# Capped expert layer with added rows, experts and combination as one program, and the last layer's stores issued from SyncE

## The chip, the cores and the metric

The kernel runs on one core of one Trainium2 chip. The metric is the device time of one execution in microseconds. Three runs of the kernel before gave 2523.3, 2524.7 and 2529.2 us, median 2524.7.

## The reference

A two-layer network on x of 32 x 64 = 2048 tokens of 256 float32 numbers. Six blocks are added to x in turn, each on the layer-normed x: attention over a compressed context, a state-space block, the **capped** mixture of experts, cross attention, self attention, and a second mixture (the **last layer**). The change touches the two mixtures:

```python
# capped: E=64 experts of width 176, K=6, CAP=128, a shared expert of width 352
scores = softmax(xf @ gate_w.T); _, idx = top_k(scores + gate_b, K)
weights = take_along_axis(scores, idx, 1)
# rows of an expert beyond its first 128 are dropped (pos < CAP)
h  = silu(xb[e] @ w1[e].T) * (xb[e] @ w3[e].T); yb = h @ w2[e].T
y  = zeros.at[tok].add(yb[slot] * weights);  z = silu(xf@ws1.T) * (xf@ws3.T) @ ws2.T
return y + z
# last: E=64 of width 128, K=8 out of 4 of 8 groups, no cap, weights normalised,
# a shared expert of width 128; same sum
```

## The kernel before

Tokens lie as 16 tiles of 128 rows in X (SBUF). Each stage is one or more programs; at the end of each, all engines meet. `stage_moe` builds both mixtures, each as three programs.

**Routing** (`r`, L1082 to L1359). VectorE normalises a tile, SyncE stores it to memory (xn), TensorE transposes it, ScalarE copies it out twice (xnT for the shared expert, xts for the logits), TensorE makes the logits. Two buffers alternate. VectorE then chooses the K experts of all tiles (MAX8, FIND_INDEX8) and writes one-hot rows `oh` (L1298); TensorE counts them with triangular and all-ones matrices (ranks, L1173); VectorE adds over the tiles (L1303), picks each choice's slot (L1320, L1321), and the **table** is made: for each of 16 x K pairs VectorE writes `atp` (L1337), VectorE or ScalarE writes `atb` (L1339, L1218, L1224, L1226, L1341) and TensorE adds the product (L1184). Out come `tok`, the token of each slot, and in the capped layer `dest`, the row k*2048 + token of its result; empty slots have token 0 and an out-of-range `dest`.

**Experts** (`x`, L1362 to L1518). A block is 128 slots of one expert: 64 blocks in the capped layer, 192 in the last one, of which those behind the filled ones are empty. Per block: SyncE loads the weights (w13, w2) eight blocks ahead (L1387 to L1390; in the last layer a register load of the expert's number first, L1386); GpSimd gathers the rows (L1406); TensorE transposes (L1433), multiplies to hidden (L1444) and to output (L1455; in the last layer L1458 behind a register load, L1457); ScalarE copies rows (L1469) and applies silu (L1475); VectorE multiplies (L1504) and copies the result to `yb` (L1514). The result goes to memory: in the capped layer by GpSimd's indirect scatter, six blocks later in its order (L1413), in the last layer from ScalarE's queue (L1483), behind a wait for `yb`. `in_steps` writes the order: within a step, the parts of later blocks stand first (turn b+2, hidden b+1, output b; on ScalarE rows b+2, gate b+1, store b).

**Combination** (`c`, L1521 to L1641). TensorE makes the shared expert's hidden rows in units of 128 x 512 (12 in the capped layer, 4 in the last; L1564) and its outputs per tile (L1578). VectorE makes the weights (L1609, L1611 and some small ones), adds the shared output (L1630), and for each tile K multiply-adds of the results (L1634), in the capped layer also the statistics of the next norm (L1641). The results come by plain loads (capped, L1544) or by indirect gathers on GpSimd, eight a tile, three tiles of buffers (last, L1553). SyncE stores the output (L1538).

In `stage_mla` SyncE clears the capped layer's result area of 12288 rows in 16 stores (L422).

Of the kernel before, what the change touches and what calls it, by code (L numbers as in the profile page):

```python
# [44 lines left out]
SLOTS0 = E * CAP0  # L45
NB1 = T * K1 // P + E
SLOTS1 = NB1 * P
# [24 lines left out]
def bc(ap, shape):  # L72
    return ap.broadcast_to(shape)
# [124 lines left out]
def stage_mla(nc, e, d):  # L198
# [12 lines left out]
    with st.ctx:  # L211
# [36 lines left out]
        NCL = 16  # L248
        clear = sb("clear", [P, T * K0 * D // (P * NCL)])
        y_clear = d["y0"].rearrange("(n p r) d -> n p (r d)", n=NCL, p=P)  # L250
# [164 lines left out]
        with nc.Block() as block:  # L415
            @block.sync
            def _(sp):

                for n in range(NCL):
                    if n < NT - 3:  # L420
                        sp.wait_ge(sem("x_added"), n + 1)
                    sp.dma_start(y_clear[n], clear[:, :]).then_inc(sem("y_clear"), 16)  # L422
                sp.wait_ge(sem("y_clear"), 16 * NCL)

# [623 lines left out]
def stage_moe(nc, e, d, layer):  # L1048
# [16 lines left out]
    xn, y = d[f"xn{layer}"], d[f"y{layer}"]  # L1065
    R = 8

    with st.ctx:
        xnT = sb("xnT", [P, KD, T])
        gslot = None if capped else sb("gslot", [P, NT, K], U32)  # L1070
        wts = sb("wts", [P, NT, K])
        tok = sb("tok", [P, NB_], U32)
        dest = sb("dest", [P, NB_], U32) if capped else None
        ebrow = sb("ebrow", [1, NB_], U32)
        ws13, ws2 = sb("ws13", [P, KD, 2, SI]), sb("ws2", [P, NSB, D])
        w2all = None if capped else sb("w2all", [P, E, D])
        sc = sb("sc", [P, NT, E])
        oh = sb("oh", [P, NT, K, E], BF16)
        slotf = sb("slotf", [P, NT, K])


        r = Stage(nc, f"m{layer}r")  # L1082
        rs = r.sem
        with r.ctx:
# [6 lines left out]
            NA = 2 * E if capped else NB_  # L1091
            ACT3 = 3
            if capped:
                destp, desti = r.sb("destp", [P, 2, NT, K]), r.sb("desti", [P, 2, NB_], I32)
                slotv = r.sb("slotv", [P, 3, NB_])
            else:
                far, ntok = r.sb("far", [P, NT, K]), r.sb("ntok", [P, NT])
                dist = r.sb("dist", [P, 2, NB_])
            ln = LayerNorm(r, e, r.ps("psT2", [P, 512]))
            xts = r.sb("xts", [P, 2, KD, P])  # L1100
# [4 lines left out]
            pr = r.sb("pr", [P, NT, K, E])  # L1105
            ltrib, onesb = r.sb("ltrib", [P, P], BF16), r.sb("onesb", [P, P], BF16)
            before = r.sb("before", [P, NT + 1, E])
            sloti = r.sb("sloti", [P, 2, NT, K], I32)
            place = r.sb("place", [P, 2, NT, K])
            HQ = 16  # L1110
            atp = r.sb("atp", [P, HQ, P], F16)
            atb = r.sb("atb", [P, HQ, NA], F16)
            nb = r.sb("nb", [P, 4, E])
            nbi = r.sb("nbi", [P, 2, E], I32)
            ebc = r.sb("ebc", [P, 2])
            gt8, gs = r.sb("gt8", [P, NT, NGR, 8]), r.sb("gs", [P, NT, NGR])
            gm = r.sb("gm", [P, NT, NGR])
# [4 lines left out]

            def by_scalar(n):

                return capped or n % ACT3 == ACT3 - 1

            def act_count(n):

                return n if capped else n // ACT3
# [4 lines left out]
            if capped:  # L1134
                LOADS.append((destp[:, :, :, :], d["dest_parts"]))
            W_ALL = 16 * len(LOADS)

            with nc.Block() as block:  # L1138
                @block.sync
                def _(sp):  # L1140
# [4 lines left out]
                    with sp.Fori(0, NT // 2) as p:  # L1145
                        for u in range(2):
                            sp.wait_ge(rs("xs_ready", u), p + 1)
                            sp.dma_start(xn.rearrange("(t p) d -> t p d", p=P)[2 * p + u], ln.xs[:, u, :]).then_inc(rs("xs_stored", u), 16)
                    for u in range(2):
                        sp.wait_ge(rs("xs_stored", u), 16 * (NT // 2))  # L1150
                    if not capped:
                        sp.dma_start(w2all[:, :, :], d["m1_w2"].rearrange("e f d -> f e d")).then_inc(rs("shared"), 16)
                    sp.wait_ge(rs("shared"), 32 if capped else 48)

                @block.tensor
                def _(pe):
                    def logits(p, u):
                        pe.wait_ge(rs("weights"), W_ALL)
                        pe.wait_ge(rs("xts", u), p + 1)
                        pe.wait_ge(rs("logits_out", u), p)  # L1160
                        for k in range(KD):
                            mm = pe.matmul(psc[:, 8 * u, :], xts[:, u, k, :], gw[:, k, :], start=(k == 0), stop=(k == KD - 1))
                        mm.then_inc(rs("logits", u), 1)

                    in_steps(pe, [lambda p, u: ln.tensor_tile(pe, p, u), logits], NT // 2, 2)

                    for u in range(2):
                        pe.wait_ge(rs("logits_out", u), NT // 2)
                    for k in range(K):
                        pe.wait_ge(rs("oh"), k + 1)  # L1170
                        for ranks, w in ((psl, ltrib), (pst, onesb)):
                            for n in range(2):
                                mm = pe.matmul(ranks[:, 8 * n:8 * n + 8, :], w[:, :], oh[:, 8 * n:8 * n + 8, k, :], start=(k == 0), stop=(k == K - 1))  # L1173
                    mm.then_inc(rs("ranks"), 1)
                    if not capped:
                        pe.wait_ge(rs("ebc"), 1)
                        for n in range(2):
                            mm = pe.matmul(ln.psT[0:1, n * P:(n + 1) * P], ebc[:, n:n + 1], ident[:, :], start=True, stop=True)
                        mm.then_inc(rs("ebt"), 1)
# [6 lines left out]

                @block.scalar
                def _(a):
                    ln.scalar_std(a)

                    def rows(p, u):
                        a.wait_ge(rs("logits", u), p)
                        ln.scalar_tile(a, p, u, xnT[:, :, bass.ds(P * (2 * p + u), P)])
                        a.activation(xts[:, u], ln.banks[u][:, 0:D].rearrange("p (k n) -> p k n", k=KD), ACT.Copy).then_inc(rs("xts", u), 1)

                    def logits(p, u):
                        a.wait_ge(rs("logits", u), p + 1)
                        carry_waits(a, rs("passed_act"))
                        a.activation(sc[:, bass.ds(2 * p + u, 1), :].rearrange("p o e -> p (o e)"), psc[:, 8 * u, :], ACT.Copy).then_inc(rs("logits_out", u), 1)

                    in_steps(a, [rows, logits], NT // 2, 2)
                    if capped:
                        a.wait_ge(rs("shifted"), 1)
                        a.activation(ex[:, :, :], sc[:, :, :], ACT.Exp).then_inc(rs("exp"), 1)
                    else:
                        for u in range(2):
                            a.wait_ge(rs("logits_out", u), NT // 2)
                        a.activation(ex[:, :, :], sc[:, :, :], ACT.Exp, scale=-1.0).then_inc(rs("exp"), 1)
                    for n in range(NT * K):
# [5 lines left out]
                        if capped:  # L1215
                            if t == 0:
                                a.wait_ge(rs("oh"), k + 1)
# [1250 lines left out]
```

## Time and profile before

| what | us |
|---|---|
| profiled execution | 2530.89 |
| its span | 2529.0 |
| busy: TensorE, VectorE | 1946.5 (77%), 1596.9 (63%) |
| busy: GpSimd, ScalarE | 1204.2 (48%), 1052.6 (42%) |
| capped layer: routing, experts, combination | 107, 196, 97 |
| last layer: routing, experts, combination | 145, 387, 177 |
| mean granted TensorE clock | 0.879 |

Times of a stage are read from the timeline, where its first and last instructions stand; a granted clock of 1.00 is 2.4 GHz and 0.50 is 1.2 GHz. A float32 product appears as two matmul records. Names are the program's with buffer numbers left out: m0r, m0x, m0c are the capped layer's three programs, m1r, m1x, m1c the last layer's.

### The profile page before, as it was taken

The numbers are of one execution on the slowest core, as the hardware profiler recorded it, in microseconds if no ns is written. First come the engines' busy times: TensorE is split into PE (matmuls) and PEld (weight loads), VectorE is DVE, ScalarE is ACT, GpSimd is POOL, SyncE is SP. The second block draws the span as 40 slices with busy tenths as digits, with TensorE's granted clock in tenths as the row PEclk, the third lists the DMA queues.
The fourth block names the chain that finished last, engine by engine and source line by source line (L and its number), as shares of the span: only waits on it lengthen the run. The fifth ranks groups of instructions, "written<-read, shape, count | busy, mean of one in ns | idle before, by whom it ended". The sixth has DMA issues, their size and how long they took to land. (4 is left out here: it accounts for less than half of the span.)

```text
span 2529.0 us, 40086 instructions
## 1 busy us (share of the span) xinstructions
PE 1946.5 (77%) x11338; PEld 1327.9 (53%) x11339; DVE 1596.9 (63%) x3459; ACT 1052.6 (42%) x3039; POOL 1204.2 (48%) x999
## 2 busy tenths in 40 slices
PE   5699967888887646998868999778635899998410
PEld 5378833343433232775436888567521777776200
DVE  6599818999999867334846777455579333332643
ACT  1367627656574234442027777433215222222000
POOL 1488606766666501774004555255300544453576
PEclk9699988999999955999969999899855899999755
DMA  7211213303030012885421111000040889899333
GB/s 214 79 67 74 99 33 133 108 27 121 14 134 1 0 59 77 264 253 159 126 67 31 35 31 31 27 2 1 26 154 1 255 277 275 276 260 225 104 115 106
DMA packets 163386, 274.38 MB, mean 108 GB/s; under 512 B 28674, under 2 KB 95339, under 8 KB 163060
## 3 DMA queue, kind: packets, MB, share of 16 engines
q1 hardware_dynamic: 108788, 186.31, 23.4%
q0 software_dynamic: 24320, 58.81, 8.9%
q10 hardware_dynamic: 30144, 27.62, 3.2%
q8 instruction: 66, 1.08, 0.2%
q14 instruction: 68, 0.56, 0.1%
HBM read 223.03 MB, written 56.90 MB: 111 GB/s over the span
## 5 line engine op out<-in xcount | busy, mean ns | idle before, releaser
L982 POOL TENSOR_TENSOR b_h<-b_h,b_bcb 128x1024 f32<-128x1024 f32 x128 | 301.8, 2358 | 151.4 <-DVE b_h L1020 150.8
L1406 POOL DMA_INDIRECT m1x_xb<-scratch_xn,m_tok x192 | 181.5, 945 | 334.9 <-PE m1x_psx L1433 166.9
L838 PE MATMUL b_psy<-b_h,ident 128*128 128x512 f32 x512 | 255.0, 625 | 75.2 <-POOL b_h L982 75.1
L1020 DVE TENSOR_TENSOR_SCAN b_h<-b_dA,b_pbx 128x1024 f32<-128x1024 f32 x128 | 292.6, 2286 | 4.4
L1504 DVE TENSOR_TENSOR m1x_hT<-m1x_sg,m1x_psh 128x128 f32<-128x128 f32 x192 | 55.3, 288 | 260.0 <-ACT m1x_sg L1475 260.0
L1444 PE MATMUL m1x_psh<-m1x_xe,m1x_w 128*128 128x128 f32 x1536 | 209.3, 280 | 10.7 <-DMA m1x_w<-in_m_w 10.6
L838 PEld LDWEIGHTS b_psy<-b_h,ident 128*128 128x128 f32 x512 | 94.7, 196 | 218.8 <-POOL b_h L982 130.4
L940 ACT ACTIVATE b_dA<-b_delta,b_A 128x504 f32<-128x504 f32 x256 | 166.8, 706 | 92.9 <-DVE b_h L1020 88.0
L1444 PEld LDWEIGHTS m1x_psh<-m1x_xe,m1x_w 128*128 128x128 f32 x1536 | 190.3, 195 | 15.4 <-DMA m1x_w<-in_m_w 7.2
L1014 DVE TENSOR_TENSOR b_pbx<-b_pdx,b_bcb 128x1024 f32<-128x1024 f32 x128 | 157.6, 1231 | 51.1 <-ACT b_pdx L924 45.1
L1768 POOL TENSOR_TENSOR x_s<-x_s,x_rs 128x1024 f32<-128x1024 f32 x64 | 121.1, 1893 | 133.7 <-DVE x_rs L1935 133.6
L1469 ACT ACTIVATE m1x_xe<-m1x_psx 128x256 f32<-128x256 f32 x192 | 73.6, 383 | 266.4 <-DVE m1x_yb L1514 256.3
L1553 POOL DMA_INDIRECT m1c_yg<-scratch_y,m_gslot x128 | 127.0, 992 | 65.2 <-issue 38.7
L1458 PE MATMUL m1x_psy<-m_w2all,m1x_hT 128*128 x384 | 134.1, 431 | 14.4 <-issue 8.0
L1406 POOL DMA_INDIRECT m0x_xb<-scratch_xn,m_tok x64 | 62.3, 973 | 137.6 <-POOLq L1138 118.4
L1887 ACT ACTIVATE x_s<-x_s,x_nm 128x256 f32<-128x256 f32 x256 | 126.6, 501 | 0.0
L618 DVE TENSOR_TENSOR a_prod<-a_psk,a_kg 128x1024 f32<-128x1024 f32 x96 | 111.3, 1215 | 15.9 <-POOL a_kg L445 15.4
L1925 DVE CUSTOM_DVE_ANT_0 x_s<-x_psS,x_maskr 128x256 f32<-128x256 f32 x256 | 92.4, 417 | 35.3 <-PE x_psS L1806 32.8
L1634 DVE SCALAR_TENSOR_TENSOR X<-m1c_yg,m_wts,X 128x256 f32<-128x256 f32 x128 | 62.6, 489 | 81.8 <-DMA m1c_yg<-scratch_y,m_gslot 77.7
L570 ACT ACTIVATE a_prod<-a_prod 128x128 f32<-128x128 f32 x384 | 112.5, 299 | 2.3 <-DVE a_prod L618 2.3
L453 POOL TENSOR_TENSOR a_ol<-a_probs,a_kg 128x1024 f32<-128x1024 f32 x48 | 90.0, 1902 | 40.1 <-DVE a_probs L651 40.1
L1578 PE MATMUL m1c_pso<-m_ws,m1c_hs 128*128 128x256 f32 x32 | 17.4, 658 | 106.5 <-DVE X L1630 95.3
(421 smaller groups left out, 4590.4 us busy)
## 6 DMA issues: line engine op xcount, KB each, us to landing
m1x_w<-in_m_w SPq DMA_DIRECT2D x192, 256.0 KB, 4.4
b_bcb<-scratch_bc_rows SPq DMA_DIRECT2D x64, 512.0 KB, 4.8
scratch_y<-m1x_yb ACTq DMA_DIRECT2D x192, 128.0 KB, 4.2
m0x_w<-in_m_w SPq DMA_DIRECT2D x64, 368.0 KB
scratch_y<-a_clear SPq DMA_DIRECT2D x16, 768.0 KB, 3.2
m0c_yg<-scratch_y SPq DMA_DIRECT2D x16, 768.0 KB, 4.6
a_c<-in_ctxT SPq DMA_DIRECT2D x16, 512.0 KB, 3.7
m0x_w<-in_m_w SPq DMA_DIRECT2D x64, 128.0 KB
```

Of the source, the lines that this page charges most:

```text
L570: ins = a.activation(w, w, ACT.Copy, accum_out=raw[:, t % 2, b, j, h:h + 1])
L838: mm = pe.matmul(psy[:, k % 2, :], ident[:, :], h[:, u % HB, j, :], start=False, stop=(nq == NQ - 1 and j == CQ - 1))
L940: ins = a.activation(dA[:, u % DB, j, :].rearrange("p (b l) -> p b l", b=NB)[:, :, 1:S], dv, ACT.Exp, scale=A[:, c, n:n + 1])
L982: q.tensor_tensor(hs, hs, bcb[:, 1, CQ * nq:CQ * nq + CQ], ALU.mult).then_inc(sem("hc"), 1)
L1014: v.tensor_tensor(pbx[:, :, :], bc(pdx[:, (NCH * g + c) % 2, None, :], [P, CQ, GT]), bcb[:, 0, CQ * nq:CQ * nq + CQ], ALU.mult).then_inc(s ...
L1020: v.tensor_tensor_scan(h[:, u % HB].rearrange("p j n -> p (j n)"), dA[:, u % DB].rearrange("p j n -> p (j n)"), pbx[:, :, :].rearrange("p ...
L1406: g.indirect_dma_start(out=xb[:, j, :], out_offset=None, in_=xn, in_offset=bass.IndirectOffsetOnAxis(ap=tok[:, b:b + 1], axis=0)).then_inc ...
L1444: mm = pe.matmul(psh[u][0:CW[n], n, :], w13[:, j, k, lo:lo + CW[n]], xe[:, u, k, :], start=(k == 0), stop=(k == KD - 1))
L1458: mm = pe.matmul(psyy[u][:, 0:D], hT[:, u, 0, :], w2all[:, bass.ds(b, 1), :].rearrange("p o d -> p (o d)"), start=True, stop=True)
L1553: g.indirect_dma_start(out=yg[:, u, k, :], out_offset=None, in_=y, in_offset=bass.IndirectOffsetOnAxis(ap=gslot[:, t, k:k + 1], axis=0)).t ...
L1768: g.tensor_tensor(half, half, bc(rs_[:, b % 2, 4 * h:4 * h + 4, None], [P, 4, SK]), ALU.mult).then_inc(sem("probs"), 1)
L1887: ins = a.activation(s[:, b % 2, hp, :], s[:, b % 2, hp, :], ACT.Exp, bias=nm[:, b % 2, hp:hp + 1], scale=ISC, accum_out=sm[:, b % 2, hp:h ...
```

## The change

- The capped layer adds its weighted results in memory. `dest` is now the token's own row; the scatter has `compute_op=add` and goes to one of three totals (block modulo 3), each behind the landing of the one before on the same total; the totals have 128 spare rows for empty slots. The scores are stored behind the rows of xn (1280 B a row), gathered with them, and VectorE multiplies by the score's column when it copies to yb.
- The capped layer has 16 block buffers for 8, the scatter stands 12 blocks behind the gather for 6, and its first 16 weight blocks are loaded in routing.
- Experts and combination are one program in both mixtures. The shared units: capped 2 before the ranks, 5 behind them, 3 ahead of the experts, 2 behind; last 2 and 2. hs holds all tiles.
- Behind the capped experts VectorE adds the shared outputs, then three totals a group of four tiles.
- Routing: one copy of the transposed rows; four row buffers for two; the choice in two halves of eight tiles; in the capped layer ScalarE writes two of three `atb`, of 64 columns for 128.
- The last layer's stores move from ScalarE's queue to SyncE's, behind each block's weight load, and GpSimd's gather waits for yb, no more for the transposes.
- The cleared area is three totals of 2176 rows, in six stores.

The core of the diff:

```diff
+    R, XR = 16 if capped else 8, 4
+    UNITS = NSB * NG
+    FIRST, SECOND = (2, 7) if capped else (2, 4)
...
@@ routing, sync
+                    for t in range(NT):
+                        sp.wait_ge(rs("xr"), t + 1)
+                        sp.dma_start(xn[P * t:P * t + P, 0:D], xr[:, t % XR, :]).then_inc(rs("xr_stored", t % XR), 16)
+                    if capped:
+                        for j in range(R):
+                            expert_weights(sp, j, j)
...
+                        sp.wait_ge(rs("scores"), 2)
+                        sp.dma_start(xn[:, D:D + E].rearrange("(t p) e -> p t e", p=P), sc[:, :, :]).then_inc(rs("scores_stored"), 16)
@@ routing, tensor
+                    for m in range(FIRST):
+                        units(m)
+                    pe.wait_ge(rs("hs"), FIRST)
+                    for n in range(2):
+                        for k in range(K):
+                            pe.wait_ge(rs("oh"), K * n + k + 1)
...
+                    for m in range(FIRST, SECOND):
+                        units(m)
@@ routing, who writes atb
-                return capped or n % ACT3 == ACT3 - 1
+                return n % 3 != 2 if capped else n % 3 == 2
@@ experts, sync
+                    def store(p, j):
+                        sp.wait_ge(xs("yb", j % 2), used(p, j) + 1)
+                        sp.dma_start(y.rearrange("(b p) d -> b p d", p=P)[bass.ds(R * p + j, 1)].rearrange("o p d -> (o p) d"), yb[:, j, :]).then_inc(xs("y_stored", j), 16)
...
                     with sp.Fori(0, NR - 1) as p:
                         for j in range(R):
                             sp.wait_ge(xs("y_done", j % 2), used(p, j) + 1)
                             weights(p + 1, j)
+                            if not capped:
+                                store(p, j)
...
+                        for s in range(NSUM):
+                            sp.wait_ge(xs("y_added", s), 16 * len(range(s, NB_, NSUM)))
+                        for g in range(NG):
+                            if g >= RB:
+                                sp.wait_ge(xs("summed"), NSUM * (g - RB + 1))
+                            for s in range(NSUM):
+                                sp.dma_start(yg[:, g % RB, s, :, :], totals[s].rearrange("(t p) d -> p t d", p=P)[:, 4 * g:4 * g + 4, :]).then_inc(xs("yg", g % RB), 16)
@@ experts, gpsimd
                         if n:
-                            g.wait_ge(xs("xb", j), 16 * n)
-                            g.wait_ge(xs("xb_used", j), n)
+                            g.wait_ge(xs("yb", b % 2), (b - R) // 2 + 1)
+                            if capped:
+                                g.wait_ge(xs("y_added", (b - R) % NSUM), 16 * ((b - R) // NSUM + 1))
...
+                        s, n = b % NSUM, b // NSUM
                         g.wait_ge(xs("yb", b % 2), b // 2 + 1)
-                        g.indirect_dma_start(out=y, out_offset=bass.IndirectOffsetOnAxis(ap=dest[:, b:b + 1], axis=0), in_=yb[:, j, :],
-                                             in_offset=None, bounds_check=T * K - 1, oob_is_err=False).then_inc(xs("y_stored", j), 16)
+                        if n:
+                            g.wait_ge(xs("y_added", s), 16 * n)
+                        g.indirect_dma_start(out=totals[s], out_offset=bass.IndirectOffsetOnAxis(ap=dest[:, b:b + 1], axis=0), in_=yb[:, b % R, :],
+                                             in_offset=None, compute_op=ALU.add).then_inc(xs("y_added", s), 16)
@@ experts, tensor
+                    for m in EARLY:
+                        units(m)
                     in_steps(pe, [turn, hidden, output], NR, R)
+                    for t in range(NT):
+                        if t % 2 == 0 and t // 2 < len(LATE):
+                            units(LATE[t // 2])
+                        shared_output(t)
@@ experts, scalar
-                    in_steps(a, [rows, gate] if capped else [rows, gate, store], NR, R)
+                    in_steps(a, [rows, gate], NR, R)
@@ experts, vector
+                        if capped:
+                            v.tensor_scalar(yb[:, j, :], psyy[u][:, 0:D], xb[:, j, bass.ds(R * p + j + D, 1)], None, ALU.mult).then_inc(xs("yb", u), 1)
...
+                    v.wait_ge(xs("x_added"), NT)
+                    for g in range(NG) if capped else ():
+                        xg = X[:, 4 * g:4 * g + 4, :]
+                        v.wait_ge(xs("yg", g % RB), 16 * NSUM * (g // RB + 1))
+                        for s in range(NSUM):
+                            v.tensor_tensor(xg, xg, yg[:, g % RB, s, :, :], ALU.add).then_inc(xs("summed"), 1)
+                            v.wait_ge(xs("summed"), NSUM * g + s + 1)
+                        for t in range(4 * g, 4 * g + 4):
+                            v.bn_stats(e["stats"][:, t, :], X[:, t, :]).then_inc(xs("next_bn"), 1)
```

Here `EARLY` is units 7 to 9 and `LATE` units 10 and 11 in the capped layer, both are empty in the last one; `units` makes one unit into a single pair of banks behind the gate of the unit before; `shared_output` makes a tile's shared output into one of four banks; `expert_weights` is the three weight loads of a block as before. In the last layer the weights `wts` are made by VectorE behind the shared outputs, and the gathers and multiply-adds follow as before.

## Rows read from the trace of the kernel before

**Rows 1.** Windows by stage: length, busy us of each engine, granted clock, DMA share, GB/s.

```profile
887.00:994.00 107.00, 57.40 (x216) 32.05 (x216) 82.60 (x331) 47.00 (x148) 0.11 (x1) 0.55 0.11 35
994.00:1190.00 196.00, 180.97 (x1152) 136.83 (x1152) 64.25 (x192) 77.38 (x206) 127.29 (x128) 0.96 0.80 231
1190.00:1287.00 97.00, 72.50 (x193) 39.48 (x194) 82.06 (x159) 8.64 (x14) 0.00 (x0) 0.82 0.44 136
1965.00:2352.00 387.00, 356.01 (x2304) 295.51 (x2304) 123.81 (x384) 108.70 (x385) 181.47 (x192) 0.98 0.90 260
2352.00:2529.00 177.00, 37.18 (x64) 16.38 (x64) 89.58 (x162) 2.39 (x4) 127.04 (x128) 0.57 0.37 108
```

**Rows 2.** The page: a DMA queue's packets, MB and share; the chain that ended last.

```profile
q0 software_dynamic: 24320, 58.81, 8.9%
POOL m1c_yg L1553 5%; DVE X L1634 0%; DMA m1c_yg<-scratch_y,m_gslot 0%; POOLq L1532 0%; DVEq L1632 0%; POOLq L1380 0%
```

**Rows 3.** Timeline, capped combination: start us, length us, engine, line, operation.

```profile
1182.54 1.32 PE L1455 MATMUL m0x_psy<-m0x_w,m0x_hT 128*128 128x256 f32 x4 [0.21 <-DVE m0x_hT L1507]
...
1190.29 9.05 PE L1564 MATMUL m0c_pgu<-m_xnT,m_ws 128*128 128x512 f32 x16 [6.43 <-PEq L1380]
1222.87 2.76 PE L1578 MATMUL m0c_pso<-m_ws,m0c_hs 128*128 128x256 f32 x12
1230.19 3.60 PE L1564 MATMUL m0c_pgu<-m_xnT,m_ws 128*128 128x512 f32 x8
...
1282.31 0.43 DVE L1641 BATCH_NORM_STATS2 stats<-X 128x6 f32<-128x256 f32 x1
```

**Rows 4.** Groups by line, capped combination: busy us, mean ns, idle before.

```profile
L1634 DVE SCALAR_TENSOR_TENSOR X<-m0c_yg,m_wts,X 128x256 f32<-128x256 f32 x96 | 46.6, 485 | 3.4
L1606 DVE TENSOR_TENSOR m0c_hs<-m0c_sgs,m0c_pgu 128x512 f32<-128x512 f32 x8 | 5.3, 679 | 2.8 <-ACT m0c_sgs L1588 2.8
```

**Rows 5.** Windows inside the two expert stages, columns as in Rows 1.

```profile
1060.00:1120.00 60.00, 59.28 (x387) 44.77 (x385) 20.69 (x63) 27.41 (x70) 42.89 (x43) 1.00 0.88 252
2000.00:2050.00 50.00, 48.08 (x318) 39.67 (x317) 17.09 (x54) 14.41 (x53) 24.86 (x27) 1.00 0.89 280
2250.00:2300.00 50.00, 43.90 (x286) 35.84 (x284) 15.81 (x49) 13.68 (x48) 22.67 (x24) 1.00 1.00 220
```

**Rows 6.** Groups by line, capped experts, GpSimd.

```profile
L1413 POOL DMA_INDIRECT scratch_y<-m0x_yb,m_dest x46 | 47.0, 1021 | 25.0 <-issue 12.7 <-DVE m0x_yb L1514 12.3
L1406 POOL DMA_INDIRECT m0x_xb<-scratch_xn,m_tok x46 | 44.9, 975 | 14.0 <-issue 11.0 <-DVE m0x_yb L1514 3.0
```

**Rows 7.** Timeline: capped routing, start and drain of the last layer's experts.

```profile
961.67 24.71 ACT L1218 ACTIVATE m0r_atb<-m_oh,m0r_destp 128x64 f16<-128x64 bf16 x80 [20.34 <-PE m0r_psc L1184]
...
1966.62 1.45 SPq L1387 DMA_DIRECT2D m1x_w<-in_m_w  x2
...
2343.20 0.69 PE L1458 MATMUL m1x_psy<-m_w2all,m1x_hT 128*128 x2
...
2346.55 0.69 PE L1458 MATMUL m1x_psy<-m_w2all,m1x_hT 128*128 x2
```

**Rows 8.** Waits, last layer's experts, 2000 to 2320 us: total us, times, longest.

```profile
ACT m1x_xe L1469 <- DVE m1x_yb L1514: 222.7, 164, 1.7
PEld m1x_psy L1458 <- issue: 37.1, 135, 0.5
...
SPq L1386 <- PE m1x_psy L1458: 105.7, 161, 3.1
```

**Rows 9.** The final gathers' tile: duration ns min/median/max, first and last start.

```profile
L1553 POOL DMA_INDIRECT m1c_yg<-scratch_y,m_gslot x128: 942/946/1966, 2354.0 to 2518.8; - x128
```

**Rows 10.** Groups by line, capped routing, VectorE.

```profile
L90 DVE BATCH_NORM_STATS2 stats<-X 128x6 f32<-128x256 f32 x16 | 5.3, 412 | 1.3 <-PEq L2347 1.3
L1263 DVE TENSOR_TENSOR m0r_sel<-m_sc,m0r_gb 128x1024 f32<-128x1024 f32 x1 | 1.2, 1224 | 0.0
```

**Rows 11.** The capped layer's scatters (L1413), issue to landing.

```profile
DMA to landing us min/median/max: 2.1/3.7/4.7
```

More of the change, by code:

```diff
@@ L1064, in stage_moe @@
     NSB = len(SBW)
-    xn, y = d[f"xn{layer}"], d[f"y{layer}"]
-    R = 8
+    xn = d[f"xn{layer}"]
+    totals = [d[f"y{layer}{n}"] for n in range(NSUM)] if capped else None
+    y = None if capped else d["y1"]
+    R, XR = 16 if capped else 8, 4
+    UNITS = NSB * NG
+    FIRST, SECOND = (2, 7) if capped else (2, 4)
     with st.ctx:
+        tok, dest = sb("tok", [P, NB_], U32), sb("dest", [P, NB_], U32)
+        ebrow = sb("ebrow", [1, NB_], U32)
+        gslot = None if capped else sb("gslot", [P, NT, K], U32)
+        ws13, ws2 = sb("ws13", [P, KD, 2, SI]), sb("ws2", [P, NSB, D])
@@ L1167, in _ @@
[L1167 to L1173, printed above, removed]
+                            mm = pe.matmul(psc[:, t, :], xnT[:, k, P * t:P * t + P], gw[:, k, :], start=(k == 0), stop=(k == KD - 1))
@@ new lines, in logits, with units @@
+                        mm.then_inc(rs("logits"), 1)
+                    def units(m):
+                        pe.wait_ge(rs("shared"), 32)
+                        if m > FIRST:
+                            pe.wait_ge(rs("sel"), 1)
+                        if m >= 2 and m != FIRST:
+                            pe.wait_ge(rs("hs"), m - 1)
+                        shared_products(pe, m, *gate_up(m))
+                    turn(0)
+                    for t in range(1, NT):
+                        turn(t)
+                        logits(t - 1)
@@ new lines, in _ @@
+                    logits(NT - 1)
+                    for m in range(FIRST):
[4 more added lines that the diff above has]
+                            pe.wait_ge(rs("oh"), K * n + k + 1)
+                            for ranks, w in ((psl, ltrib), (pst, onesb)):
+                                mm = pe.matmul(ranks[:, HN * n:HN * n + HN, :], w[:, :], oh[:, HN * n:HN * n + HN, k, :], start=(k == 0), stop=(k == K - 1))
@@ L1189, in _ @@
                     ln.scalar_std(a)
[L1191 to L1208, printed above, removed]
+                    for t in range(NT):
+                        a.wait_ge(rs("turned"), t + 1)
+                        a.activation(xnT[:, :, P * t:P * t + P], psT[t % 2][:, 0:D].rearrange("p (k n) -> p k n", k=KD), ACT.Copy).then_inc(rs("xnT"), 1)
+                        if t == (HN + 5 if capped else HN + 1):
+                            exps(a, 0)
+                    exps(a, 1)
+                    for m in range(SECOND):
+                        shared_silu(a, m, gate_up(m)[0])
                     for n in range(NT * K):
@@ L1240, in _ @@
                     ln.vector_stats(v)
[L1241 to L1245 removed]
+                    for t in range(XR):
+                        normed(t)
                     v.wait_ge(rs("weights"), W_ALL)
@@ L1290, in _ @@
[L1290 to L1298 removed]
+                    step(v.memset(before[:, 0, :], 0.0))
@@ L1610, in _ @@
-                    step(ins)
-                    step(v.tensor_reduce(wts[:, :, :], pr[:, :, :, :], AX_X, ALU.add))
-                    if not capped:
+                        ins.then_inc(xs("chain"), 1)
+                        v.wait_ge(xs("chain"), n_step[0])
+                    n_step = [0]
+                    for m in EARLY:
+                        shared_gated(v, m, pgu[1])
+                    in_steps(v, [gated, outputs], NR, R)
+                    for t in range(NT):
+                        if t % 2 == 0 and t // 2 < len(LATE):
+                            shared_gated(v, LATE[t // 2], pgu[1])
+                        v.wait_ge(xs("out"), t + 1)
+                        v.tensor_tensor(X[:, t, :], X[:, t, :], pso[t % 4][:, 0:D], ALU.add).then_inc(xs("x_added"), 1)
```

509 lines of the change are left out of this document (246 added, 263 removed).

## The prediction

> **What bounds the kernel now.** I read the windows by stage first. One core runs six stages in a row, so a gain in one is a gain in the time. The change touches the capped layer (routing 887 to 994 us, experts to 1190, combination to 1287) and the last layer (experts 1965 to 2352, final combination to 2529, its routing before them) [rows 1]. The page's chain covers only the end: the final gathers on GpSimd [rows 2].
>
> Capped combination: from the last expert product (ends 1183.9) to the last statistics (end 1282.7) are 98.9 us [rows 3]. VectorE is busy 82.1 of 97 there [rows 1], 46.6 of it in 96 multiply-adds [rows 4].
>
> Capped experts: 387 TensorE records in 60 us, 18 a block, are 2.79 us a block, with TensorE never idle [rows 5]. GpSimd needs a gather and a scatter, 0.98 + 1.02 and two issue gaps of 0.30: 2.60 a block, just not the bound [rows 6]. DMA is at 0.88 of 16 engines and 252 GB/s.
>
> Capped routing: the table's 96 steps take 0.31 us each (80 in 24.7), paced by VectorE, which makes two writes in each [rows 7]; TensorE is near 1.2 GHz, a clock of 0.55 [rows 1].
>
> Last layer's experts: 12 records a block, 318 in 50 us, are 1.89 us a block [rows 5]. ScalarE idles 1.36 us a block waiting for yb: the store stands ahead of the next row copy in its program, and so do, behind it, the copy, the gate, VectorE's product and the load of the block's expert number on TensorE. That load ends late: TensorE's weight loads stand idle 37.1 us over 164 blocks at the output, 0.23 us a block [rows 8]. In the drain of the last blocks outputs follow at 1.68 us (two blocks in 3.35) [rows 7].
>
> The final gathers: 128 at 0.95 us and a gap of 0.30, GpSimd all the way [rows 9].
>
> **The change part by part, on the profiled execution (2530.9 us, span 2529.0; the median, 2524.7, is 6.2 below it).**
>
> *Combination of the capped layer.* Results are weighted as they leave PSUM and accumulated into three totals in memory, so the multiply-adds and the weights' products and reduction go. What is left behind the experts: 2 shared units at 3.44 and 16 shared outputs at 1.38 at most (two took 2.76 end to end, 1.30 start to start) = 27.7 us on TensorE at 2.4 GHz, where the experts leave it [rows 3]; 0.9 for the last add; then 12 additions of 128x1024 at 1.22 + 0.04 and 16 statistics at 0.33 to 0.35: 20.7 [rows 10]. Sum 49.3 against 98.9: **-49.6**. The 6 MB of totals load meanwhile: nine loads of 512 KB at 250 to 280 GB/s take 17 to 19 us, behind the last scatter (about +7 us), the first third long before +28.6. The weighting is VectorE's copy with a factor; VectorE is busy only 64 of 196 us in the stage [rows 1]: 0.
>
> *Accumulating scatters.* No row shows one. GpSimd's instruction: below, the plain one's 1.02 us; above, the longest indirect one of the trace, 1.97 us [rows 6, 9]. I take 1.02 to 1.1, the same kind of instruction with the same rows. At 1.97 GpSimd needs 3.55 us a block, falls 50 us behind, and some 14 of it lie under the shared outputs: +36. Landing: the plain one's is 3.7 us (2.1 to 4.7) [rows 11]; each waits for the one three blocks earlier, so up to 3 x 2.79 - 1.3 = 7 us it is free. I take 5. Gathers run twelve blocks ahead and wait for a scatter issued four blocks before: free.
>
> DMA load: the software queue moved 58.8 MB [rows 2]; its gathers are 384 x 131 KB + 48 x 65 KB = 53.5, so scatters were 5.3 MB of a possible 8.4 (empty slots weren't written). Now all 8.4 are, gathers (1280 B a row for 1024) add 2.1, and 16 of 64 weight blocks (8.9 MB) move into routing, where DMA is at 0.11. The stage falls from 45 MB to 42, at 0.80 share before: 0, TensorE stays the bound. The Trainium skill (Collectives: The Full Stack, "The bandwidth ceiling: the fold count and why AG ≠ RS ≠ AR") says that an add in the DMA path needs two source reads, twice a copy's read descriptors. By it the stage would move some 50 MB, 174 us at its 288 GB/s per full share, still under 190: the sum stays, the margin goes.
>
> *Weights ahead, early units.* From the first gather (993.9) to the stage's end were 190.0 us, 64 x 2.79 = 178.6 and 11.4 of start and drain. Now three shared units stand first, one buffer deep: two in 9.05 (clock rising from 1.2 to 2.4 GHz), one in 3.44 [rows 3], two turnarounds of silu and gate at up to 0.68 each [rows 4] and 0.5 of hand-overs = 3.8, then 0.8 to the first product and 1.4 of drain: 18.5. The wait for weights goes. Net **+7**; bounds +2 to +12.
>
> *Routing, capped.* The table: ScalarE writes 64 of 96 at 0.31, 19.8; VectorE 96 + 32 at 0.155, half a step, 19.8; before 96 x 0.31 = 29.7: -9.9 [rows 7]. Three closing operations for eight: -1.1. The choice in halves starts some 5 us sooner, beside the last logits; but the rank products share banks with the first two shared units and wait for them, so they end where they did; seven gates of 0.68, five of them behind the ranks, and smaller pieces add 5. Together **-6**. If the five units there run at 1.2 GHz (6.8 us each) they end last: +4. Below, -10. Four buffers of normalised rows for two, as the store stays in the loop: taken as 0. The 48 weight loads stand on SyncE's queue behind the row stores and ahead of the scores' store; that one is awaited only at the block's end. Half the cleared bytes of the first stage (6.7 MB for 12.6) go from under compute: 0.
>
> *Routing, last layer.* Same moves, but the table is unchanged, and two more gates come on VectorE, which is the bound: **-1** (-4 to +3), by the smaller brother of the sum above.
>
> *Stores from SyncE.* ScalarE's wait for yb goes; the 0.23 us gap closes, and TensorE could run at 1.66, as in the drain. Then two others are late. DMA: 524 KB a block at 280 / 0.89 = 315 GB/s is 1.67 us [rows 5]. SyncE: two weight issues with their register loads stand 1.11 us apart where nothing holds them [rows 7]; a store adds 0.34 and some 0.2 of registers and waits: 1.65 to 1.8. Behind its new wait for yb stand the next weights; it idled 0.66 us a block [rows 8], and eight blocks of depth cover it at first, not for 150 blocks. I take 1.77 over 150 blocks: **-18**. The last 32 blocks are empty ones, and DMA is full there (1.00 at 220 GB/s) [rows 5]: 0. Bounds: 1.65 gives -36; nothing, 0. The gather's release moves from the transposes to yb, two blocks later: six blocks (10 us) are left for 1 of issue and 5 of landing: 0.
>
> On where it is issued, the Trainium skill (DMA: Bandwidth & Descriptors, "Issuing engines are not separate DMA queues") says that another issuing engine only saves sequencer time, usually small beside the DMA. By it this part is worth nothing unless that sequencer stood in the loop.
>
> *Final combination.* Shared outputs come sooner, weights later: the first multiply-add at about +29 after the last product (16 adds 9, products and reductions 19, rest 1) instead of +25. GpSimd has three buffers, 30 us of gathers and 4 of slowing beside VectorE's products, so it doesn't wait; 128 x 1.25 stay: 0 (-2 to +6).
>
> Sum: -49.6 + 7 - 6 - 1 - 18 = -67.6. Profiled execution 2463; median 2524.7 - 67 = **2458**.
>
> **The rivals.** A. *SyncE or DMA takes the whole gain of the stores* (the second page's rule comes to the same): 1.89 stays. For: SyncE's sum reaches 1.8. Against: its 0.66 us of idle. Time 2476.
> B. *GpSimd becomes the capped layer's bound*: an accumulate costs it 1.3 to 1.97 us, or lands after 7 to 9. For: only 0.19 us a block is free. Time 2470 to 2494.
> C. *Slower than before*: accumulates land so late that the chain of every third scatter rules. At landing L a block takes (L + 1.3)/3; 64 blocks less 178 of TensorE and 14 of cover must lose 67, from L = 11 us on. At 12: 283 - 192 = +91, so 2549. Against: 4.7 at most here, at 0.88 of the DMA.
> D. *TensorE-bound last experts*, 1.65: 2440.
> E. *The totals don't pay in full*: the shared outputs run at 1.2 GHz, +28: 2486.
>
> **How the numbers follow.** Forecast 0.48, A 0.14, B 0.16, C 0.04, D 0.12, E 0.06. 8 in 10 lie between D with a little more from routing, 2434, and B's upper end, 2494. 0.2% (5 us) is what a measurement can tell from no change. Only C, and A, B and E together, are not faster: faster 0.94, same 0.01, slower 0.05.
>
> **What would show it.** Capped layer: from last expert product to last statistics about 49 us; 12 additions of 1.22; table 20 us; first hidden product 17 us after the first gather; blocks at 2.79 with scatters landing under 7. Last layer: ScalarE no longer waits for yb, no idle before the output's weights, 1.77 a block, SyncE seldom idle; final gathers 165 us. I am wrong if GpSimd waits for its own scatters, or if the block time there stays 1.89.

## The result, and the profile after

The changed kernel takes 2453.2 us (median of 4 runs, 2451.8 to 2458.1) against 2525.7 for the kernel before in the same runs: 0.9715 of it, 95% interval 0.9697 to 0.9733. Forecast were 2458 and a range of 2434 to 2494. The profiled execution took 2452.9, its span 2451.3, so the two spans differ by 77.7 us, some 5 of which are the profiled execution of before standing above its median.

Windows by stage of the changed kernel, columns as in [rows 1]: capped routing, experts, combination, then the last layer's experts and final combination.

```profile
887.00:983.00 96.00, 71.55 (x273) 42.35 (x274) 78.19 (x290) 32.90 (x93) 0.00 (x0) 0.71 0.42 137
983.00:1176.00 193.00, 188.87 (x1176) 138.77 (x1175) 69.56 (x194) 60.98 (x195) 151.56 (x120) 0.99 0.92 231
1176.00:1226.00 50.00, 28.13 (x114) 20.93 (x112) 28.57 (x47) 1.19 (x2) 12.43 (x8) 0.82 0.58 150
1903.00:2276.00 373.00, 342.12 (x2306) 291.40 (x2307) 130.61 (x384) 126.78 (x384) 182.69 (x192) 0.99 0.91 270
2276.00:2451.00 175.00, 6.70 (x32) 5.55 (x30) 89.41 (x168) 0.00 (x0) 124.64 (x128) 0.53 0.37 109
```

The combination is down from 97 us to 50. The experts' DMA share rose from 0.80 to 0.92 at the same 231 GB/s: the same rate costs the engines more. The timeline of the capped layer (start, length, instruction) has the marks from which its terms are read:

```profile
961.00 20.34 PE L1254 MATMUL m0r_psc<-m0r_atb,m0r_atp 128*128 128x64 f16 x96 [2.16 <-DVE m0r_atp L1425]
...
983.35 0.98 POOL L1514 DMA_INDIRECT m0x_xb<-scratch_xn,m_tok  x1 [108.06 <-POOLq L1178]
...
999.09 1.57 PE L1561 MATMUL m0x_psh<-m0x_xe,m_w 128*128 128x128 f32 x12 [0.57 <-issue]
...
1174.97 1.32 PE L1572 MATMUL m0x_psy<-m_w,m0x_hT 128*128 128x256 f32 x4 [0.21 <-DVE m0x_hT L1633]
...
1189.06 1.55 POOL L1523 DMA_INDIRECT scratch_y<-m0x_yb,m_dest  x1 [0.30 <-issue]
...
1193.05 16.80 SPq L1499 DMA_DIRECT2D m_w<-scratch_y  x12
...
1204.62 3.74 DVE L1665 TENSOR_TENSOR X<-X,m_w 128x1024 f32<-128x1024 f32 x3
...
1223.64 1.41 DVE L1668 BATCH_NORM_STATS2 stats<-X 128x6 f32<-128x256 f32 x4
```

The table takes 20.3 us. From the last expert product (1176.3) to the last statistics (1225.05) are 48.8 us, against 98.9 of [rows 3]. From the first hidden product to the last output are 177.2 us, 2.77 a block. One thing does not show in the total: GpSimd's last scatter ends 14.3 us after the last product, and its tile says why (duration min/median/max in ns):

```profile
L1523 POOL DMA_INDIRECT scratch_y<-m0x_yb,m_dest x64: 1546/1582/1625, 1004.2 to 1189.1; - x64
```

An accumulating scatter holds GpSimd 1.58 us, not the 1.02 of [rows 6]. With the gather and two gaps that is 3.18 us a block against TensorE's 2.77; GpSimd falls behind all through the stage. It still costs nothing: SyncE starts to load the totals at 1193.05, the loads land within 6.3 to 7.8 us, and VectorE first adds them at 1204.62. Some 4 us are left over.

In the last layer's experts ScalarE no longer waits for `yb`; TensorE now waits for weights (waits of 1920 to 2240 us: total, times, longest):

```profile
ACT m1x_xe L1607 <- PE m1x_psx L1550: 94.7, 170, 1.0
...
PE m1x_psh L1561 <- DMA m1x_w<-in_m_w: 16.0, 29, 1.2
...
PEld m1x_psy L1575 <- issue: 12.4, 49, 0.5
```

The idle time ahead of the output's weights fell from 37.1 [rows 8] to 12.4 us, and a new one came. SyncE's instructions by line say from where: the register load of the expert's number (L1474), the weight issue (L1089), the store (L1479), duration min/median/max in ns.

```profile
L1474 SPq FUSED_REGOPS  x376: 46/152/188, 1902.5 to 2261.7; - x188
L1474 SPq TENSOR_LOAD <-m_ebrow x192: 262/269/617, 1902.0 to 2261.4; - x192
L1474 SPq SEQ_ASSERT  x192: 18/18/37, 1902.8 to 2261.9; - x192
...
L1089 SPq DMA_DIRECT2D m1x_w<-in_m_w x192: 337/338/931, 1903.0 to 2262.1; - x192
...
L1479 SPq DMA_DIRECT2D scratch_y<-m1x_yb x192: 332/356/1251, 1914.0 to 2276.3; - x192
L1479 SPq FUSED_REGOPS  x184: 46/46/51, 1913.8 to 2262.5; - x184
L1479 SPq MOVE scratch_y<-m1x_yb x184: 29/29/29, 1913.9 to 2262.6; - x184
```

With the same 46 and 29 ns at the weight issue, a block's instructions are 0.27 + 0.20 + 0.02 + 0.07 + 0.34 + 0.07 + 0.36 = 1.33 us; with ten short gaps between them it is 1.72 to 1.87, as SyncE's timeline has the stores 1.83, 1.72, 1.81 and 1.87 us apart:

```profile
2049.77 0.36 SPq L1479 DMA_DIRECT2D scratch_y<-m1x_yb  x1
2051.07 0.34 SPq L1089 DMA_DIRECT2D m1x_w<-in_m_w  x1
2051.60 0.35 SPq L1479 DMA_DIRECT2D scratch_y<-m1x_yb  x1
2052.79 0.34 SPq L1089 DMA_DIRECT2D m1x_w<-in_m_w  x1
2053.32 0.36 SPq L1479 DMA_DIRECT2D scratch_y<-m1x_yb  x1
2054.60 0.34 SPq L1089 DMA_DIRECT2D m1x_w<-in_m_w  x1
2055.13 0.36 SPq L1479 DMA_DIRECT2D scratch_y<-m1x_yb  x1
...
2057.00 0.35 SPq L1479 DMA_DIRECT2D scratch_y<-m1x_yb  x1
```

Once in eight blocks the loop turns, and two stores stand 2.2 us apart or more; eight blocks take 14.8 us in the middle of the stage, 1.85 each.

```profile
2089.97 0.36 SPq L1479 DMA_DIRECT2D scratch_y<-m1x_yb  x1
2091.64 0.35 SPq L1089 DMA_DIRECT2D m1x_w<-in_m_w  x1
2092.18 0.35 SPq L1479 DMA_DIRECT2D scratch_y<-m1x_yb  x1
```

The view of SyncE's own waits from 1920 to 2240 us is empty: where it idled 0.66 us a block [rows 8], it now never waits.

So three things were to be tested: whether the stores' move is what shortened the stage and SyncE what limits it; what the addition in the scatter costs and what hides it; and what the shared units put in early are worth.

### The profile page after: what moved, and what is told of

It is laid out like the page before. It is cut to its first block and busy times, and to the rows that moved or that the text cites. A ratio compares the mean times of both kernels' runs of the same rounds, so it can differ in the third digit from the quotient of the medians.

```text
span 2451.3 us, 38904 instructions
## 1 busy us (share of the span) xinstructions
PE 1893.5 (77%) x11338; PEld 1313.0 (54%) x11339; DVE 1558.4 (64%) x3359; ACT 1027.6 (42%) x2932; POOL 1240.4 (51%) x999
## 3 DMA queue, kind: packets, MB, share of 16 engines
q8 instruction: 69, 1.13, 0.2%
## 5 line engine op out<-in xcount | busy, mean ns | idle before, releaser
L1540 POOL DMA_INDIRECT m1x_yg<-scratch_y,m_gslot x128 | 124.6, 974 | 55.5 <-issue 38.7
L1685 DVE SCALAR_TENSOR_TENSOR X<-m1x_yg,m1x_wts,X 128x256 f32<-128x256 f32 x128 | 62.3, 488 | 82.2 <-DMA m1x_yg<-scratch_y,m_gslot 78.1
L1523 POOL DMA_INDIRECT scratch_y<-m0x_yb,m_dest x64 | 101.0, 1578 | 24.1 <-issue 15.9
```

Of the source, the lines that this page charges most:

```text
L1540: g.indirect_dma_start(out=yg[:, u, k, :], out_offset=None, in_=y, in_offset=bass.IndirectOffsetOnAxis(ap=gslot[:, t, k:k + 1], axis=0)).t ...
```

## The experiments

Twelve runs in three groups of four, each group on one chip with runs of the kernel before. That one took 2530.8, 2529.9 and 2590.5 us there, so kernels are compared within a group or, in the first two, by their ratio to it; the changed kernel's own ratio was 0.9715 at first and 0.9682 here, so across groups 8 us can't be told apart. Each time is a median of five runs or six.

**The changed kernel again.**

> The changed kernel itself, timed beside the next three on one chip so that they can be compared with it: 2453 us, ratio to the kernel before 0.9715, if the chips agree. A block of the last layer's experts takes 1.82 us in the middle of the stage, the accumulating scatter 1.58 us on GpSimd.

Measured: 2452.1 us, 0.9682 (0.9668 to 0.9697). It is the mark for the first eight.

**e1. Stores back on ScalarE, where they stood.** `store` itself moves along; shown are the two calls.

```
-                            if not capped:
-                                store(p, j)
...
-                    in_steps(a, [rows, gate], NR, R)
+                    in_steps(a, [rows, gate] if capped else [rows, gate, store], NR, R)
```

> The changed kernel with only the last layer's stores back on ScalarE's queue, at the place where they stood. Theory (the stores' move is what shortened that stage): the block goes back from 1.82 to 1.89 us, 150 blocks give +10.6 us, 2464 in all, and ScalarE waits for yb 1.3 us a block again. Rival (the shorter stage comes from something else in the change, the released gathers or the rows): the block stays 1.82 and the time 2453.

Measured: 2467.8 us, 15.7 more than the changed kernel. ScalarE's wait and TensorE's idle time are back:

```profile
ACT m1x_xe L1599 <- DVE m1x_yb L1639: 188.5, 144, 1.4
...
PEld m1x_psy L1567 <- issue: 37.1, 133, 0.5
```

The stage takes 385.1 us (first gather to last output), as the 385.4 of before, against 373.1 and 374.2 in two profiles of the changed kernel. The move is what shortened it, and by 11 to 12 us.

**e2. Stores on ScalarE, one step later; and the same edit alone in the kernel before (e5).** In `in_steps` an empty part moves the store one step back, behind another block's row copy and gate, where yb has long been written. The edit of e5; e2 has the same line, and the stores gone from SyncE as in e1:

```
-                    in_steps(a, [rows, gate] if capped else [rows, gate, store], NR, R)
+                    in_steps(a, [rows, gate] if capped else [rows, gate, None, store], NR, R)
```

> Stores on ScalarE's queue, but one step later in its program, so that yb has long been written when ScalarE comes to the store. SyncE has only the weights. Theory S (SyncE's program of 1.73 to 1.82 us a block sets the pace in the changed kernel): nothing is left but TensorE's own 1.65 and the DMA's 1.67 us, the block falls to 1.68 and the time by 150 x 0.14 = 21 us to 2432. Rival D (the DMA engines at 0.9 and 283 GB/s are the limit): the block stays at 1.80 or more and the time at 2450 to 2453.

> The kernel before with one edit: ScalarE's store of a block stands one step later in its program, still on ScalarE's queue. Theory (what cost time was ScalarE's wait for yb ahead of the next row copy, not the queue): the last layer's block falls from 1.89 to 1.68 us, 150 blocks give -31 us, 2498 against 2530. Rival (it is the queue or the DMA): 0.

Measured: e2 2437.0 us, 0.9626 (0.9613 to 0.9639), 15 less than the changed kernel; e5 2505.1 us, 25 less than the kernel before. The views of the DMA count the blocks in 200 us of the stage, the kernel before first (2000 to 2200), then the changed one and e2 (1983 to 2183):

```profile
scratch_y<-m1x_yb ACTq DMA_DIRECT2D x105, 128.0 KB, 3.9
```
```profile
scratch_y<-m1x_yb SPq DMA_DIRECT2D x108, 128.0 KB
```
```profile
scratch_y<-m1x_yb ACTq DMA_DIRECT2D x118, 128.0 KB
```

That is 1.90, 1.85 and 1.69 us a block. Windows of e2 and of the changed kernel, 40 us each, show the DMA beside it:

```profile
2023.00:2063.00 40.00, 40.00 (x288) 35.55 (x286) 16.28 (x48) 15.57 (x47) 22.23 (x25) 1.00 0.95 312
```
```profile
2023.00:2063.00 40.00, 38.23 (x261) 32.55 (x260) 14.97 (x44) 14.18 (x44) 20.60 (x22) 1.00 0.91 287
```

In this window of e2 TensorE has no idle time. The DMA moves 312 GB/s where it moved 287: it was not the limit. The stage takes 352.5 us, 21 less, as theory S had it; the total only 15 less. The missing 6 us lie ahead of the stage, in code without an edit: its first gather came at 1909.4 against 1901.4. Of these 8 us 5.7 lie even ahead of the capped layer, whose statistics end at 893.5 against 887.8; over all profiles with the changed code they end between 886.4 and 894.3. No run explains this spread, and a total carries it.

Between e1 and e2 only the store's place in ScalarE's program differs, and the stage goes from 385.1 to 352.5 us. In e5 it goes from 385.4 to 358.6 us; -31 was expected for the total and -25 came. So being on ScalarE's queue was not what cost time in the kernel before, but the wait ahead of the row copy.

**e8. SyncE without the register load.** Is it SyncE's instructions, or that weights and stores share a queue?

```
-                            b = sp.value_load(ebrow[0:1, bass.ds(b, 1)], min_val=0, max_val=E - 1)
+                            b = (7 * j + 3) % E
```

> The changed kernel, stores on SyncE's queue, but SyncE loads fixed experts' weights in the last layer (seven apart, eight different ones; what a block is multiplied with is left out), so that the register load of the expert number and what follows it, 0.27 + 0.15 us and gaps, go from SyncE's program. Bytes, queue and the order of its issues stay. Theory S (SyncE's own instructions, 1.73 to 1.82 us a block, set the pace): they take about 1.25, the block falls to 1.68, 21 us go in the stage: 2432 to 2437. Rival Q (weights and stores in one hardware queue are the limit, and the stores' other queue was what helped on ScalarE): the block stays at 1.82, time 2452.

Measured: 2450.4 us in the third group, where the late store took 2447.5 and e9, whose last layer is the changed kernel's, has this stage at 375.2 us. Windows of 40 us, e8 first, then e9:

```profile
2030.00:2070.00 40.00, 39.11 (x278) 34.29 (x277) 15.45 (x47) 15.18 (x46) 21.94 (x24) 1.00 0.94 300
```
```profile
2030.00:2070.00 40.00, 38.07 (x260) 32.26 (x258) 14.26 (x42) 13.97 (x43) 20.59 (x22) 1.00 0.91 280
```

12 records a block make 1.73 us against 1.85; the stage is 363.7 us against 375.2, and 355.8 and 358.1 in this group's two profiles of the late store on ScalarE. What went from SyncE's program is 0.56 us a block (0.27 + 0.20 + 0.02 + 0.07 above). With the stores still in SyncE's queue that brought 11.5 us of the 17 to 19 between the two places. Theory S holds in kind, not in full: 1.68 us a block and 21 us were expected. The other 5 to 8 us may be the shared queue or the wait for yb ahead of the weights (SyncE now waits 62 times for yb from 1920 to 2240 us, 12.1 us in all), and are open. One thing more differs: with eight fixed experts a weight packet of 2 KB takes 94 ns in the trace for 109 in e9, and what that adds to the gain was not separated.

**e4. A scatter that writes instead of adding.**

```
-                                             in_offset=None, compute_op=ALU.add).then_inc(xs("y_added", s), 16)
+                                             in_offset=None).then_inc(xs("y_added", s), 16)
```

> The capped layer's scatters write instead of adding (the sum over a token's experts is left out). All 128 rows of a block are still written. Theory A (the addition makes the instruction long): the scatter takes 1.02 us on GpSimd as in the kernel before, GpSimd needs 2.6 us a block and no longer falls behind TensorE; its share of the software queue's time falls from 4.3 to about 3.2% per MB of a 120 us stretch. Theory B (the 128 rows do, empty slots included, where before they were skipped): it stays at 1.58. In both the time stays within 2 us of 2452, because GpSimd's backlog of 14 us lies under the 28 us of shared outputs: the 0.5 us a block that were mis-sized cost nothing.

Measured: 2453.7 us, 0.9693 (0.9675 to 0.9711), no change. The scatter's tile in e4, and the software queue (packets, MB, share of 16 engines, 1010 to 1130 us) in e4 and in the changed kernel:

```profile
L1523 POOL DMA_INDIRECT scratch_y<-m0x_yb,m_dest x64: 969/987/997, 1005.4 to 1177.6; - x64
```
```profile
q0 software_dynamic: 4152, 12.73, 37.3%
```
```profile
q0 software_dynamic: 7173, 10.98, 46.3%
```

Theory A: the addition costs GpSimd 0.59 us with all 128 rows written in both; that the kernel before skips empty slots made no difference (1.02). And it costs the DMA engines: in 120 us e4 does 43.4 blocks at 2.77, the changed kernel 37.7 at 3.18, so 0.293 and 0.291 MB a block, but 1.03 and 1.47 us of 16 engines, and 96 and 190 packets. The trace's single packets divide that: a plain scatter goes as 32 packets of 4 KB at 159 ns, 0.32 us of 16 engines, an adding one as 128 of 1 KB at 107 ns, 0.86 us, 2.7 times as much. The Trainium skill (Collectives: The Full Stack, "The bandwidth ceiling: the fold count and why AG ≠ RS ≠ AR") says that the add needs two source reads. A packet of the addition takes 107 ns where the weights' packets of 1 KB take 49 beside it, which agrees with that; the moved bytes do not show the second read, and the fourfold number of packets is a cost of its own. Neither cost reached the end of the stage.

**e3 and e6. Two totals, and one.**

```
-NSUM = 3
+NSUM = 2      # e6: 1
```

> Two totals for three. Behind the experts 4 of 12 additions of 1.25 us go and 4 of 12 loads. Each scatter now waits for the one two before it. Theory (a scatter lands within 4.8 us: two blocks of GpSimd's work, 2 x 3.18, less its own 1.58): GpSimd's pace stays 3.18 a block, -5 us, 2448. Rival (it lands after 7 us or more): a block takes (7 + 1.9)/2 = 4.4 us on GpSimd, 64 blocks put its end 80 us later, of which 4 us are free: 2525 and more.

> One total: each accumulating scatter waits for the landing of the one before it. This measures the landing. By the formula of the prediction a block takes L + 1.9 us (landing counted from the instruction's end, 1.58 for the instruction, 0.3 for the wait's end): with 4 to 5.5 us, as two totals showed where GpSimd waited, 5.9 to 7.4 a block, 64 blocks last 380 to 470 us less 8 additions (10 us), and the time is 2452 + 190 to 280 = 2640 to 2730. If the landing overlaps better (2.5 us): 4.4 a block, 2540.

Measured: e3 2464.3 us, 12 more; e6 2572.5, 1.0159 of the kernel before (1.0139 to 1.0178). The tile `yb` in e6: GpSimd's idle time by what ended it, and issue to landing (min/median/max us).

```profile
L1523 POOL DMA_INDIRECT scratch_y<-m0x_yb,m_dest x64: 1545/1581/1625, 1006.2 to 1327.3; - x64
...
  DMA scratch_y<-m0x_yb,m_dest: 146.2, 60
...
DMA to landing us min/median/max: 3.7/3.8/6.5
```

An adding scatter lands 3.8 us after its issue in the median, as a plain one [rows 11], but up to 6.5. With one total they follow each other in (1327.3 - 1006.2)/63 = 5.10 us, so rival C's mechanism is real, and makes the kernel slower than before with one total for three. My expectation took 5.9 to 7.4 and was too high. With two, the combination fell by the four additions, from 48.7 to 43.7 us, but GpSimd waited for landings 17 times (tile `yb`, e3):

```profile
  DMA scratch_y<-m0x_yb,m_dest: 17.5, 17
```

and the last expert product came 12.7 us later after the first gather (206.9 against 194.2 in the profile of the changed kernel run beside it). I had allowed landings of 4.8 us and expected all or nothing; the median is below that, the tail is not.

**e7. One shared unit ahead of the experts for three.**

```
-    EARLY, LATE = (range(SECOND, SECOND + 3), range(SECOND + 3, UNITS)) if capped else ((), ())
+    EARLY, LATE = (range(SECOND, SECOND + 1), range(SECOND + 1, UNITS)) if capped else ((), ())
```

> One shared unit ahead of the first expert block instead of three, two more behind the last. TensorE's work is the same. Theory (the first gathers cover 5.5 us, so units two and three delay the first expert block, and at the end they stand beside GpSimd's backlog): TensorE's total is the same, only the turnarounds between early units (1.4 us each) go, -1 to -3 us, 2450. Rival (GpSimd sets the end: its first scatter starts 10 us sooner, so the last one ends sooner): nothing more, since the additions wait for TensorE. Rival L (the capped layer's expert blocks then outrun GpSimd's gathers and wait): 0 to +8.

Measured: 2461.0 us, 0.9729 (0.9713 to 0.9745): 7 more than e4 beside it, 4 to 12 more than the changed kernel by its two ratios. The spans narrow that: from the first gather to the last statistics e7 takes 246.0 us, the changed kernel 241.7 and 242.9, e4 241.0, so the edit costs 3 to 5 us, and rival L is right. TensorE comes to the first hidden product 5.6 us after the first gather for 15.7 and then waits for GpSimd's gathers (waits of 1010 to 1175 us, e7, then the changed kernel as run again):

```profile
PEld m0x_psx L1550 <- DMA m0x_xb<-scratch_xn,m_tok: 14.6, 20, 1.5
```
```profile
PEld m0x_psx L1550 <- DMA m0x_xb<-scratch_xn,m_tok: 3.0, 3, 2.0
```

The 64 blocks take 184.7 us for 177.2 (178.5 as run again), and two units more lie behind them. So GpSimd's 3.18 us a block is hidden by two things: the three units that I had booked as a delay, and the shared outputs behind the last product, which cover its last 14 us.

**e9 and e10. Fewer and more units beside the routing.** e9 has one for five behind the ranks; e10 has six, together with the late store, and stands against the late store alone, run beside it.

```
-    FIRST, SECOND = (2, 7) if capped else (2, 4)
+    FIRST, SECOND = (2, 3) if capped else (2, 4)      # e10: (2, 8), the gates' range one longer
```

> One shared unit beside the capped layer's rank sums and slots for five; three still stand ahead of the experts, and six for two behind them. Behind the experts that adds 4 x 3.44 = 13.8 us. Theory of the prediction (the gates of these units, 0.68 each, and their waits cost the routing some 5 us): the routing gets 3 us shorter, +11, 2463. Rival (they lie free beside VectorE's work and TensorE's idle time, as the table's unchanged start 74 us into the stage says): nothing comes back, +14, 2466.

> The late store on ScalarE and one more shared unit beside the capped routing (six for five), one fewer behind the experts. TensorE's five units end 2 us before the table starts, so a sixth (3.6 us) and its gate delay the table by 1.5 to 3 us, and 3.4 go behind the experts: -2 to 0 against the late store alone, 2435 to 2437. If a unit beside the routing delays the table by its whole length, +1.

> The late store on ScalarE again, beside the last one on one chip: 0.9626 of the kernel before, 2437 us.

Measured in the third group: e9 2476.4, e10 2446.0, the late store again 2447.5 us. In e9's profile the combination is 62.4 us for 48.8, +13.6, and the routing (last statistics to first gather) 88.6 for 91.0, -2.4: four units beside the routing cost it 0.6 us each and save 3.4 each. Together that is +11.2, as the theory had it. The changed kernel itself was not timed in this group; e9 is 29 above the late store, of which 15 are the stores' (e2). In e10 the sixth unit delays the table by 3.8 us and saves 3.5 behind the experts: nothing is left to fill. The 1.4 us between e10's and the late store's medians lie inside the spread of either.

The version that beats both kernels is e2, the late store: 0.9626 of the kernel before in the first group, 0.9445 (0.9417 to 0.9472) in the third.

## Why the prediction was right, by its steps

| step | predicted | measured in the spans |
|---|---|---|
| combination of the capped layer | -49.6 | 98.9 to 48.8: -50.1 |
| weights ahead, early units | +7 | 190.0 to 192.9: +2.9 |
| routing, capped | -6 | 101.4 to 91.0: -10.4 |
| routing, last layer | -1 | 146.0 to 141.5: -4.5 |
| stores from SyncE | -18 | 385.4 to 373.1: -12.3 |
| final combination | 0 | 178.4 to 175.5: -2.9 |
| other stages | 0 | -0.4 |
| sum | -67.6 | -77.7 |

The capped routing is counted from the end of its statistics, the last one from its first instruction. The medians moved by 72.5 us.

- **Combination.** Right in every part: two units and 16 outputs at 2.4 GHz end at +28.3 for 28.6, an addition takes 1.25 us, the statistics 0.35. No run takes this part back by itself; its terms were moved one by one, four additions fewer for 5.0 us (e3) and four units more for 13.6 (e9).
- **Accumulating scatters.** This is the step that failed, without touching the total: 1.58 us is in the bounds of 1.02 to 1.97, and I took the lower end since the instruction looked the same. By the prediction's own formula 1.58 makes 3.16 us a block, 24 us behind and 14 of them covered, so +10; that it came to 0 is luck, for the cover of the three units stood nowhere in the sum. "TensorE stays the bound" is true only with three units ahead (e7) and some 4 us of spare time before the first addition. The condition of rival B came about (1.3 to 1.97 us), its price did not. The landing, taken as 5 us, is 3.8 in the median of e6, and the DMA share rose where I had it fall.
- **Early units.** 15.7 us to the first hidden product for 17 forecast, blocks of 2.77 for 2.79.
- **Capped routing.** The table (29.6 to 20.3) and the closing (3.0 to 2.0) came as computed. "+5" for gates was the mis-sized term: the ranks ended 3 us sooner, since the first eight tiles' one-hot rows were ready, and the gates took 2.8 back (e9: 0.6 a unit), so the table starts at the same 74 us into the stage.
- **Last routing.** The same, larger: the ranks' products end 66.5 us into the stage, for 72.9, and gates and closing gave back 1.9. I had said "the smaller brother"; the choice in halves is longer there, so starting half of it early is worth more. How much is less sure: in the other profiles of the same code this routing takes 141.5 to 144.0 us.
- **Stores.** The mechanism is right to both sides (e1, e5), and rival A's took a third of the gain: SyncE's sum, put at 1.65 to 1.8, is 1.72 to 1.87 and 1.85 with the turn of the loop, so the block is 1.83 to 1.85 and not 1.77. I counted two weight issues from a place outside the loop. The Trainium skill (DMA: Bandwidth & Descriptors, "Issuing engines are not separate DMA queues") says that another issuing engine only saves sequencer time, usually small; here the sequencers were the loop, and the same stores on three places cost 1.90, 1.85 and 1.69 us a block.
- **Final combination.** The slow gathers beside VectorE's products are shorter (longest 1.13 us for 1.97), which I had left out.

Of the other rivals, D's 1.65 us a block was held off by the stores in SyncE's program (e2 has 1.69), C needs fewer totals, and E's shared outputs ran at 2.4 GHz, one in 1.30 us.

The errors partly cancel: routing and early units were 12.0 us better than forecast, the stores 5.7 worse.

## What to carry to other kernels

When a step is moved to another engine's program, add up that program's every instruction, register work and gaps included; where the sum comes near the block time, keep it on its engine and move it to where its wait has long ended. Where an instruction is another one with a flag more, take bounds for its cost and not the other's cost; and where the cost is covered, find the cover and its size, since a later "improvement" may take it away. Work put into an engine's idle time beside another's chain cost a fifth of its length here (e9), until the idle time was full (e10).

## What the runs showed of the hardware

- An indirect scatter of 128 rows of 1 KB holds GpSimd 0.99 us, with an addition 1.58; both land 3.7 to 3.8 us after the issue in the median. The addition goes as 128 packets of 1 KB for 32 of 4 KB and takes the DMA engines 0.86 us for 0.32.
- At a DMA share of 1.01 and 1.06 (two windows of 60 us from 1000 us on) TensorE was busy all 60 us of each, and over the stage VectorE's product and ScalarE's silu kept their lengths (288 ns for 289, 277 for 277): the capped block stayed at 2.77 us.
- A turn of SyncE's loop costs time: seven of eight blocks take 1.72 to 1.87 us there, the eighth 2.2 to 2.5.
- The kernel before was 2.4% slower in the third group than in the others, the late store 0.4%. No profile of the kernel before from that group shows where. The late store's two profiles differ by 8.1 us, 5.7 more in the last experts and 4.0 in the final combination, which takes 184 to 185 us for 175.5 in e8 to e10 as well; why stays open.
